# Two 16-head cross-attention stages: score products regrouped from four heads on 96 rows to two heads on each 64-row half, and softmax sums inverted after a turn

## The reference

```python
q = (layernorm(x) @ Wq.T + bq) -> [B=32, 16, 56, 8]      # biases and mask in L1 only
k = (ctx @ Wk.T + bk)          -> [B, 16, 1500, 8]
v = (ctx @ Wv.T + bv)          -> [B, 16, 1500, 8]
scores = einsum('bhqd,bhkd->bhqk', q, k) / sqrt(8)
scores = where(mask == 0, -1e9, scores)                   # L1 only
out = einsum('bhqk,bhkd->bhqd', softmax(scores), v)
x = x + out.reshape(B, 56, 128) @ Wo.T + bo
```

## Time and profile before

| | |
|---|---|
| median of 3 runs | 3891.91 us (3890.11 to 3892.72) |
| the profiled execution | 3887.87 us, its span 3886.1 us |
| mean granted PE clock | 0.935 of 2.4 GHz |
| busy share of the span: PE, PEld, DVE, ACT, POOL | 86%, 63%, 65%, 53%, 30% |
| exps of L1, of L2: first to last | 436.4 to 1232.8 us, 1552.2 to 2348.3 us |
| DMA issues on SP: keys from k_hi, from k_lo | 256 and 128 for each of L1 and L2, 187.5 KB each |

### The profile page before, as it was taken

The page is one execution under the profiler, slowest core; times in us unless marked ns, Lnnn a source line. Parts: engine busy times, 40 slices in busy tenths (PEclk is TensorE's granted clock), DMA queues, the critical chain, the costliest instruction groups (busy, mean ns, idle before and its releaser), DMA issues. The chain is left out here.

```text
span 3886.1 us, 96641 instructions
## 1 busy us (share of the span) xinstructions
PE 3344.9 (86%) x40650; PEld 2451.9 (63%) x40650; DVE 2514.8 (65%) x3568; ACT 2066.9 (53%) x3842; POOL 1154.1 (30%) x1125
## 2 busy tenths in 40 slices
PE   6776799999998575999999996579999999999988
PEld 4455577777776563777777774346666666666654
DVE  5633577677774224777777773667878878778751
ACT  3211366566664111666566663367677776776733
POOL 0012312222121214222222111135455455554520
PEclk9877899999999686999999997689999999999989
DMA  7932666555561314555554530100000000000000
GB/s 226 254 120 72 176 165 167 157 150 157 162 167 31 106 38 116 129 132 133 124 124 123 129 92 7 22 24 17 25 25 17 24 18 23 25 17 25 17 1 26
DMA packets 137255, 345.88 MB, mean 89 GB/s; under 512 B 56179, under 2 KB 79547, under 8 KB 136827
## 3 DMA queue, kind: packets, MB, share of 16 engines
q1 hardware_dynamic: 134139, 334.22, 32.3%
...
## 5 line engine op out<-in xcount | busy, mean ns | idle before, releaser
L2040 POOL TENSOR_TENSOR l_S<-l_S,l_shift 125x448 f32<-125x448 f32 (+1 forms) x416 | 461.1, 1147 | 329.0 <-ACT l_shift L2272 326.5
L1338 ACT ACTIVATE L1a_probs<-ps 125x448 f32<-125x448 f32 x768 | 383.2, 544 | 202.8 <-PE ps L1238 189.5
L1338 ACT ACTIVATE L2a_probs<-ps 125x448 f32<-125x448 f32 x768 | 382.9, 544 | 203.3 <-PE ps L1238 189.9
L1371 DVE TENSOR_REDUCE L2a_chunk_max<-ps 112x1 f32<-112x1000 f32 x256 | 300.9, 1196 | 147.4 <-PE ps L1197 147.0
L1371 DVE TENSOR_REDUCE L1a_chunk_max<-ps 112x1 f32<-112x1000 f32 x256 | 300.9, 1196 | 135.9 <-PE ps L1197 135.4
L2150 PE MATMUL ps<-l_S,l_z 125*128 125x448 f32 x768 | 344.3, 545 | 0.0
L2253 ACT ACTIVATE ctx_stats<-ps 125x512 f32<-125x512 f32 (+1 forms) x416 | 248.3, 597 | 180.0 <-PE ps L2098 170.8
L2317 DVE TENSOR_REDUCE l_norms<-ctx_stats 125x8 f32<-125x512 f32 (+1 forms) x416 | 268.1, 675 | 77.9 <-ACT ctx_stats L2253 77.8
L2343 DVE SCALAR_TENSOR_TENSOR l_S<-ps,l_neg_cols,l_inv_norms 125x448 f32<-125x448 f32 x384 | 256.1, 679 | 81.8 <-PE ps L2119 77.1
L1197 PE MATMUL ps<-L1a_keys,L1a_queries 98*112 98x500 f32 x768 | 264.6, 427 | 47.0 <-DVE L1a_chunk_max L1371 20.5
L1197 PE MATMUL ps<-L2a_keys,L2a_queries 96*112 96x500 f32 x768 | 264.6, 427 | 45.8 <-DVE L2a_chunk_max L1371 20.5
...
## 6 DMA issues: line engine op xcount, KB each, us to landing
L1a_keys<-L1a_k_hi SPq DMA_DIRECT2D x256, 187.5 KB
L2a_keys<-L2a_k_hi SPq DMA_DIRECT2D x256, 187.5 KB
a_ctx_T<-in_ctx_T SPq DMA_DIRECT2D x32, 750.0 KB, 11.7
L1a_ctx_T<-in_ctx_T SPq DMA_DIRECT2D x32, 750.0 KB, 6.1
xn<-L_valid SPq DMA_DIRECT2D x32, 750.0 KB, 7.6
L1a_keys<-L1a_k_lo SPq DMA_DIRECT2D x128, 187.5 KB
L2a_ctx_T<-in_ctx_T SPq DMA_DIRECT2D x32, 750.0 KB, 6.4
L2a_keys<-L2a_k_lo SPq DMA_DIRECT2D x128, 187.5 KB
```

Source lines behind the costliest of these rows:

```text
L1338: nc.scalar.activation(probs[t % NPR][:, h * HQ // 2:(h + 1) * HQ // 2], s.ps[0:KP, i % 3, 0:HQ // 2], ACT.Exp).then_inc(probs_made, 1)
L1371: ins = nc.vector.tensor_reduce(chunk_max[:, n, 0:1], product, AX.XY, ALU.max)
L2040: nc.gpsimd.tensor_tensor(S[b % 2][0:r, t, :], S[b % 2][0:r, t, :], shift[0:r, :], ALU.add)\
```

## The change

It keeps G = 4 groups but puts two heads on rows 0 to 63 and two on rows 64 to 127 (HALF = 64, GR = 16, KQ = 48, KS = 52 or 50). Each half is a block of its own with its own mask and maxima rows, and holds 2 x 56 = 112 query columns. Every 500-column row score is a pair of products, one in each half of the PE rows, into two banks; each 125 x 448 score tile is four products of 125 x 112, and the two halves' tiles are issued together (8 products, alternating halves, into two of the three banks), after which both exps are released. The pair waits for `probs_made` i - 1, where before each half waited for i - 2.

On SP each copy is cut in two, since a half takes 16 rows: 24 copies of 16 x 1500 instead of 12 of 32 x 1500 for the keys, 2 instead of 1 for the mask rows, 6 instead of 3 for the q terms, and 4 instead of 2 for the maxima. Bytes stay the same.

On POOL the queries are spread in one instruction of 112 x 896 instead of four of 96 x 224. On DVE all 12 reductions have the form 112x2 <- 112x1000. The sums are no longer spread and then inverted as 128 x 224: two small products turn them to 112 x 8 ("sums"), DVE inverts those and widens them to 112 x 256, and a step item "spread" at step 7 multiplies by the identity to bring them to 128 x 224, which DVE multiplies into `acc` straight from PSUM.

```diff
-    G, HPG = 4, 4
-    GR, GC4 = HPG * DK, HPG * SQ
+    G = 4
+    HALF = D // 2
+    GR = 2 * DK
     KQ = 3 * GR
...
-    PIECES = 12
+    ROWS = G * NKC
+    PIECES = 2 * G * 3
+
+    def half(u, n):
+
+        return slice(u * HALF, u * HALF + n)
...
+    step_items[7].append(("spread", -1, 0))
...
             def load_terms(b):
...
                 for k in range(3):
-                    sp.dma_start(q_terms[b % 2][k * GR:(k + 1) * GR, :, :],
-                                 q_dram[k, :, b * SQ:(b + 1) * SQ].rearrange("(g r) q -> r g q", g=G))\
-                        .then_inc(terms_loaded[b % 2], 16)
+                    terms = q_dram[k, :, b * SQ:(b + 1) * SQ].rearrange("(g u r) q -> u r g q", g=G, u=2)
+                    for u in range(2):
+                        sp.dma_start(q_terms[b % 2][u * HALF + k * GR:u * HALF + (k + 1) * GR, :, :], terms[u])\
+                            .then_inc(terms_loaded[b % 2], 16)
 
             def move_keys(b):
...
+                def move(u, g, k, part):
+                    first, row = (2 * g + u) * GR, u * HALF + k * GR
+                    sp.dma_start(keys[b % NKB][row:row + GR, g, :].bitcast(F32), part[first:first + GR, :].bitcast(F32))\
+                        .then_inc(keys_moved, 16)
...
                 for g in range(G):
-                    for k in (0, 2):
-                        sp.dma_start(keys[b % NKB][k * GR:(k + 1) * GR, g, :].bitcast(F32),
-                                     k_hi[g * GR:(g + 1) * GR, :].bitcast(F32)).then_inc(keys_moved, 16)
+                    for u in range(2):
+                        for k in (0, 2):
+                            move(u, g, k, k_hi)
                 sp.wait_ge(k_lo_made, b * 2 + 2)
                 for g in range(G):
-                    sp.dma_start(keys[b % NKB][GR:2 * GR, g, :].bitcast(F32),
-                                 k_lo[g * GR:(g + 1) * GR, :].bitcast(F32)).then_inc(keys_moved, 16)
+                    for u in range(2):
+                        move(u, g, 1, k_lo)
 
             def move_maxima(b):
...
                 for k, part in enumerate((max_hi, max_lo)):
-                    sp.dma_start(queries[b % NQ][SHIFT + k:SHIFT + k + 1, :, :].bitcast(F32), part[:, b % 2, :].bitcast(F32))\
-                        .then_inc(row_moved, 16)
+                    for u in range(2):
+                        row = u * HALF + SHIFT + k
+                        sp.dma_start(queries[b % NQ][row:row + 1, :, :].bitcast(F32),
+                                     part[u * G:(u + 1) * G, b % 2, :].bitcast(F32)).then_inc(row_moved, 16)
...
             def score_rows(item):
...
-                for half, (r, k) in enumerate(halves_of_row(n)):
-                    mm = nc.tensor.matmul(s.ps[0:RW, bank(item) + half, 0:KC],
-                                          queries[b % NQ][0:SHIFT, r // 2, r % 2 * RW:(r % 2 + 1) * RW],
-                                          keys[b % NKB][0:SHIFT, r // 2, k * KC:(k + 1) * KC], start=True, stop=True)
+                g, k = n // NKC, n % NKC
+                for u in range(2):
+                    mm = nc.tensor.matmul(s.ps[0:RW, bank(item) + u, 0:KC], queries[b % NQ][half(u, SHIFT), g, :],
+                                          keys[b % NKB][half(u, SHIFT), g, k * KC:(k + 1) * KC], start=True, stop=True)
...
-            def scores(b, t, h):
-                i = (b * KT + t) * 2 + h
+            def scores(b, t):
+
+                i = (b * KT + t) * 2
...
-                else:
-                    pe.wait_ge(probs_made, i - 2)
-                for g in (2 * h, 2 * h + 1):
-                    mm = nc.tensor.matmul(s.ps[0:KP, i % 3, g % 2 * GC4:(g % 2 + 1) * GC4],
-                                          keys[b % NKB][:, g, t * KP:(t + 1) * KP], queries[b % NQ][:, g, :],
-                                          start=True, stop=True, skip_group_check=True)
-                mm.then_inc(scores_made, 1)
+                if i >= 2:
+                    pe.wait_ge(probs_made, i - 1)
+                for g in range(G):
+                    for u in range(2):
+                        mm = nc.tensor.matmul(s.ps[0:KP, (i + u) % 3, g * RW:(g + 1) * RW],
+                                              keys[b % NKB][half(u, KS), g, t * KP:(t + 1) * KP],
+                                              queries[b % NQ][half(u, KS), g, :],
+                                              start=True, stop=True, skip_group_check=True)
+                        if g == G - 1:
+                            mm.then_inc(scores_made, 1)
...
             def norm(item):
...
-                nc.vector.reciprocal(inv[:, :], s.ps[:, bank(item), 0:4 * SQ]).then_inc(scratch_dve, 1)
-                dve.wait_ge(scratch_dve, by_dve[item])
                 nc.vector.tensor_tensor(heads_out[:, :, b * SQ:(b + 1) * SQ], acc[:, :].rearrange("p (c q) -> p c q", c=4),
-                                        inv[:, :].rearrange("p (c q) -> p c q", c=4), ALU.mult).then_inc(normed, 1)
+                                        s.ps[:, bank(item), 0:4 * SQ].rearrange("p (c q) -> p c q", c=4), ALU.mult)\
+                    .then_inc(scratch_dve, 1)
```

153 lines of the change are left out of this document (88 added, 65 removed).

## The result

| | before | after |
|---|---|---|
| median, lowest to highest of 4 runs | 3891.01 us, 3884.15 to 3892.72 | 4479.12 us, 4471.46 to 4486.25 |
| ratio after to before, 95% interval | | 1.1515, 1.149 to 1.154 |
| profiled span, mean granted clock | 3886.1 us, 0.935 | 4474.0 us, 0.824 |
| L1, L2: us a batch (batches 3 to 29) | 25.46, 25.42 | 34.24, 33.81 |
| clock in these batches of L1, L2 | 0.997, 1.000 | 0.758, 0.772 |

The change costs 588 us, where 250 had been forecast, and the time lies above the range (3850 to 4260). A batch is 8.8 us longer in L1 and 8.4 in L2. By the starts of the exps, the 29 periods of both stages (batches 0 to 28) take 493 us more in all, the last three batches of both 60 us more, and the first exps of the two stages come 34 us later in all.

A forecast was written before the change was run, and what follows sets the result against it. PE bounded the stages before; afterwards SP's loop over the context would, at 30.2 us a batch in L1 and 29.3 in L2 against 25.3. +142, +116, -18 and +10 make +250 on 3892: 4142 us, range 3850 to 4260.

The forecast's parts named there:

- the loop: Closed cycle from maxima over key copies, context, keys product and scores to next maxima: 23.1 us now, 30.2 and 29.3 forecast.
- SP's part, step by step: SP's queue: 24 key copies at 0.63 us, 16.1 in all; context issued 19.9 us after the maxima in L1, 19.0 in L2.
- The landing: Context load from issue to arrival: 4.8 us as a lone load, instead of 6.1 behind queued key copies.
- the tail: From the keys product's start to the end of the maxima's split: 4.5 us, plus 1.0 for the clock.
- The other value of this step: Issue cost on SP by the skill's 50 ns dispatch: 18 more DMAs add 0.9 us to the loop, giving 3809 us.
- Clock: PE waits 8 us a batch, so part of the work after the wait runs at 1.2 GHz: 1.0 us added a batch.
- the sum: Forecast total: L1 +142, L2 +116, last three batches -18, first batches +10; +250 on 3892 gives 4142 us.
- PE's part: PE's row items and score products both halve side by side, 5.4 us less a batch; PE at 20 to 21 us.
- The last three batches: Each stage's last batches, without copies ahead, get PE's saving: 3 us each, -18 us in all.
- The first exps: Start of each stage: first batches wait for a longer key list, some 5 us a stage, +10 us.
- Rivals: Cheap 16-row issues, 0.17; halves not side by side, 0.09; PE's saving in full, 0.02; gain and loss cancel, 0.03.
- rival 2: Halves do not run side by side and PE bounds: 30.5 us a batch, +322, 4214 us; chance 0.09.

The follow-up runs named there:

- cut copies: The kernel before with every copy of SP's loop cut in two (24 key copies, 4 maxima, 2 mask rows, 6 q terms), nothing else; 4258.7 us.

## Why the prediction was wrong

The sign and the costs on SP's queue were right, the size was not. The sign was right in part by luck: the loop alone does cost 362 us (cut copies), but in the changed kernel it is hardly on the path.

- **SP's part, step by step: right in what the copies cost.** A key copy was taken at 0.60 us and has a median of 0.589; the context's issue at 19.9 us after the maxima, and came at 19.5 (20.2 with cut copies alone). The landing was taken at 4.8: 4.8 with cut copies alone, 5.8 in the changed kernel. As the sole bound this loop gives 31.3 and 31.0 us a batch (cut copies alone), against the forecast's 30.2 and 29.3; the tail is what was short, 6.3 us on the average from the landing to the next maxima, where 4.5 and 1.0 stood. That the queue on the DMA engines would go was wrong: their share is 0.91 to 1.01 while the changed kernel's copies run. The other value of this step was read from the wrong place: the Trainium skill ("DMA: Bandwidth & Descriptors", Anatomy of one DMA) gives its dispatch of about 50 ns for DMAs issued from GpSimd, and these are SP's. 24 copies take 16.1 us on this queue.
- **Clock: the step that failed.** "The tail comes right after the long wait, so I add 1.0" was drawn from one late arrival in the kernel before, and it took a wait as what brings the clock down. It comes down to 0.50 for 16.5 us of each batch and costs 8.3 us, not 1.0, and in the runs it falls with no more waits than before, once the products use fewer of PE's rows: 64 rows alone lose 224 us, 50 and 52 rows 300, 32 rows 500, at 97% busy. The trace of before could not show this, since every product in its batches used 96 rows or more; the forecast never asked what a product over half of the rows does to the clock. The 29 periods of the two stages grew by 493 us instead of 258, which is 235 us of the 337 missing. In the terms of the sum, the mean batch of L1 is 19.8 (issue, 19.9 forecast) + 5.7 (landing, 4.8) + 8.7 from there to the next maxima, where 4.5 and 1.0 stood.
- **PE's part: the second step that failed.** "Both halve, 5.4 us less a batch" is not what the products do. The 5.5 and 5.2 us that were halved came from the tightest rows; over a batch of L1 rows take 6.3 and scores 7.6 us, and they save 1.6 us each, not 2.8 and 2.6. The halves do overlap (0.48 us for 8 products, 0.76 for 8 one half after the other), but a step's 896 columns now come with 8 weight loads instead of 4, and where 4 full-row products stood together they took 0.43 us. Against the 3.2 us saved stand 1.8 us more in the other products, where 0.3 had been put for the spread, and the waits: PE's gaps are 3.7 us a batch instead of 1.4, with the weight loads of scores waiting 54.8 / 17.6 = 3.1 us a batch for the exp and 1.5 for the maxima. A full-clock batch stands at 26.0 us, not at 20 to 21. The Trainium skill's speedup of up to twice for contractions of at most 64 rows ("TensorEngine Tiling (Array Packing)", Theoretical Speedup) is a bound that this trace keeps to and stays well below: 0.76 / 0.48 = 1.6 against such products in series, and 1.3 against the full-row products that they replace (13.8 us a batch of scores and rows, now 10.7).
- **The last three batches: wrong.** They were to gain 3 us each. The first two of them took 31.0 and 33.2 us in L1 and 36.0 and 34.5 in L2, instead of 23.5 and 23.0, since without copies they still have the clock (0.704 and 0.574 over the three); 60 us more in two stages, where -18 stood in the sum. The first exps came 34 us later, where +10 stood.
- **Rivals.** None of the four took place. PE bounds, as in rival 2, with few waits at L1190 (0.6 us a batch), which the prediction named as a sign against itself; but it bounds by its clock: two halves do overlap, and a pair of products of 112 columns takes 0.12 us, not over 0.2. PE's busy share is 89%, not under 80, while the clock at 0.5 in parts was there, for much longer parts. The signs that SP's wait for the maxima falls to a few us and that the DMA share stays under 1 failed too: 9.8 us, and up to 1.01.

**Open.** How copies, rows and coupled waits share the low clock: cut copies take it to 0.937 by way of the waits, rows alone to 0.861, both to 0.843, with the coupled waits to 0.661, and leaving out half of the copies brings the changed kernel from 0.758 to 0.877. The time of a mix was not the sum of its parts in any run. Whether the values in the operands weigh in it was not tried by itself, and no run shows what the clock goes by.
